# The scratch copy of queries and keys is laid out as the score stacks read it; neighbouring issues on the DMA queue are reordered

## The reference

```python
def reference(x, ...):                       # x: 8 images, 3 x 256 x 256
    gray = einsum('bchw,c->bhw', x, w)
    h = (|conv3x3(gray, scharr_x)| + |conv3x3(gray, scharr_y)|) / 2      # 8 x 256 x 256
    a = layernorm(h)                         # 8 images of 256 tokens of 256 values
    q, k, v = a@Wq+bq, a@Wk+bk, a@Wv+bv      # 16 heads of 16 values
    q, k = q@Wp, k@Wp                        # per head
    h = h + softmax(q k^T / 4) v             # per head
    n = layernorm(h); m = layernorm(n)*gamma + beta
    return h + n + 0.5*(silu(m@w1 + b1)@w2 + b2)     # w1: 256x1024, w2: 1024x256, dequantized
```

## Time and profile before

| | us |
|---|---|
| median of 3 runs (321.28, 323.62, 323.57) | 323.57 |
| the profiled execution | 326.8 |
| its span, first to last instruction | 325.1 |
| mean granted TensorE clock, share of 2.4 GHz | 0.958 |
| first stage on TensorE, until | 100.16 |
| second stage, first score by key | 104.49 |

### The profile page before, as it was taken

The page is one execution under the profiler, slowest core; times in us unless marked ns, Lnnn a source line. Parts: engine busy times, 40 slices in busy tenths (PEclk is TensorE's granted clock), DMA queues, the critical chain, the costliest instruction groups (busy, mean ns, idle before and its releaser), DMA issues.

```text
span 325.1 us, 5957 instructions
## 1 busy us (share of the span) xinstructions
PE 284.3 (87%) x2152; PEld 217.5 (67%) x2152; DVE 211.8 (65%) x421; ACT 165.7 (51%) x304; POOL 131.4 (40%) x250
## 2 busy tenths in 40 slices
PE   0599999999994999955998499879899999999996
PEld 0488888877773655533655265445699889999985
DVE  8979885947995699863699379661683563542422
ACT  1582524523331698853687379768434434444450
POOL 7533242402000058740396346217648769800000
PEclk9999999999999699995699879999999999999999
DMA  6939159671788812667064200000000100100101
GB/s 216 307 56 342 39 222 218 185 283 39 235 291 288 262 62 78 154 191 235 23 173 134 68 7 5 2 4 0 2 0 3 65 1 2 65 2 0 65 2 65
DMA packets 27215, 35.69 MB, mean 110 GB/s; under 512 B 5154, under 2 KB 16178, under 8 KB 27186
## 3 DMA queue, kind: packets, MB, share of 16 engines
q1 hardware_dynamic: 27024, 35.16, 36.1%
q10 hardware_dynamic: 162, 0.15, 0.2%
HBM read 24.42 MB, written 10.49 MB: 107 GB/s over the span
## 4 chain that ended last, share of the span: by engine, by line
PE 70%; DVE 13%; SPq 5%; DMA 4%; ACT 4%; issue 3%; ACTq 0%; DVEq 0%
PE bank L1160 42%; PE bank L1272 9%; PE bank L1252 8%; SPq L390 4%; PE bank L1230 4%; DMA qs<-negrow 3%; PE bank L1290 3%; ACT probs L1068 2%; DVE qk_l L857 2%; DVE negmax L867 1%; DVE gray L748 1%; PE bank L1298 1%; DVE xn L832 1%; PE bank L1182 1%; PE bank L1282 1%
## 5 line engine op out<-in xcount | busy, mean ns | idle before, releaser
L867 DVE TENSOR_REDUCE negmax<-bank 128x2 f32<-128x512 f32 x128 | 79.8, 683 | 26.2 <-PE bank L1230 26.1
L1068 ACT ACTIVATE probs<-bank 128x512 f32<-128x512 f32 x128 | 69.5, 595 | 39.0 <-PE bank L1252 35.9
L1252 PE MATMUL bank<-qs,ks 50*128 50x256 f32 x256 | 34.9, 354 | 21.0 <-DMA qs<-negrow 12.0
L921 DVE TENSOR_TENSOR y_l<-yf,y_h 128x512 fp32r<-128x512 f32 x32 | 23.6, 741 | 39.1 <-ACT yf L1094 39.0
L1091 ACT ACTIVATE y_h<-bank,b1col 128x512 fp32r<-128x512 f32 x32 | 22.0, 688 | 48.4 <-PE bank L1160 48.3
L1252 PEld LDWEIGHTS bank<-qs,ks 50*128 50x128 f32 x256 | 21.4, 206 | 34.9 <-DMA qs<-negrow 13.1
L1160 PE MATMUL bank<-w_h,y_h 128*128 128x256 f32 x128 | 36.9, 289 | 2.5 <-DVE y_l L921 2.1
L1272 PE MATMUL bank<-probs,vals 128*32 128x256 f32 x512 | 38.2, 421 | 0.0
L1160 PE MATMUL bank<-w_h,y_l 128*128 128x256 f32 x128 | 36.2, 282 | 0.0
L1160 PE MATMUL bank<-w_l,y_h 128*128 128x256 f32 x128 | 36.1, 282 | 0.0
L1230 PE MATMUL bank<-ks,qs 48*128 48x256 f32 x256 | 28.3, 319 | 1.6 <-DVE att L878 1.0
(11 more groups left out here) (143 smaller groups left out, 583.8 us busy)
## 6 DMA issues: line engine op xcount, KB each, us to landing
xr<-in_x SPq DMA_DIRECT2D x8, 768.0 KB, 8.2
qs<-qk_parts SPq DMA_DIRECT2D x48, 128.0 KB, 3.1
ks<-qk_parts SPq DMA_DIRECT2D x48, 128.0 KB, 3.3
qk_parts<-qk_h SPq DMA_DIRECT2D x16, 256.0 KB, 3.0
qk_parts<-qk_l SPq DMA_DIRECT2D x16, 256.0 KB, 3.0
wraw<-in_L_ffn_fc_q SPq DMA_DIRECT2D x4, 512.0 KB, 4.5
wscale<-in_L_ffn_fc_scales SPq DMA_DIRECT2D x4, 512.0 KB, 6.0
out<-osb SPq DMA_DIRECT2D x16, 128.0 KB, 1.8
```

The source lines that it names most:

```text
L867: eng.tensor_reduce(negmax[:, b % 2, u, v], entry_bank(key)[:, :].rearrange("p (t k) -> p t k", t=NT), AX.X, ALU.max, negate=True).then_in ...
L921: eng.tensor_tensor(y_l[:, p % 2, f], yf[:, n % 2], y_h[:, p % 2, f].bitcast(fp32), ALU.subtract).then_inc(s_y, 1)
L1068: eng.activation(probs[:, n % PBUF], p2[n % 3][:, :], ACT.Exp).then_inc(s_exp, 1)
L1252: ins = eng.matmul(p2[(n + v) % 3][:, t * N:(t + 1) * N], ks[rows, r, u, c + t * P:c + (t + 1) * P], qs[rows, r, u, c:c + N], start=True, ...
```

## The change

- `qk_dram` gets the shape [pair, op, part, m, v, d, u, t]. In the store the destination is walked as (u, v, d, t), 4 x 2 x 16 pieces of 2 KB, pieces of one u lying 8 KB apart; the source is 128 SBUF rows as before. In the load the source for one (m, v) is 16 rows of 8 KB, contiguous, and the destination 16 SBUF rows of 8 KB, contiguous in each row.
- `pass_neg(0, 0)` is issued ahead of all four stores of pair 3 instead of between the second and the third.
- Loads of pairs 2 and 3 are issued two a step over twelve steps (12 to 23, 28 to 39) instead of three a step over eight.
- The FFN weights of layer 1 are issued at steps 25 and 26 instead of 19 and 20, and `w2_step` and `normalise(0, .)` start three places later in `spare`: `w2_step` ends at step 44 instead of 40, `normalise(0, 5)` stands at step 52 instead of 48.

```diff
-    qk_dram = nc.dram_tensor("qk_parts", [PAIRS, 2, 2, E, COLS], fp32).ap()
+    qk_dram = nc.dram_tensor("qk_parts", [PAIRS, 2, 2, KE, 2, D, UNITS // KE, COLS], fp32).ap()
@@ store_qk
-                    eng.dma_start(qk_dram[p, op, part, m * P:(m + 1) * P, :], src[:, i, :].bitcast(fp32)).then_inc(s_store[i], 16)
+                    eng.dma_start(qk_dram[p, op, part, m].rearrange("v d u t -> u v d t"), src[:, i, :].bitcast(fp32)).then_inc(s_store[i], 16)
@@ load_qk
-                src = qk_dram[p, op, part, m * P:(m + 1) * P, :].rearrange("(u v d) t -> v d u t", v=2, d=D)[v]
-                eng.dma_start(dst[first:first + SPLIT - 2:3, r, m * 4:(m + 1) * 4, :].bitcast(fp32), src).then_inc(s_load[r][m], 16)
+                src = qk_dram[p, op, part, m, v].rearrange("d u t -> d (u t)")
+                eng.dma_start(dst[first:first + SPLIT - 2:3, r, m * 4:(m + 1) * 4, :].rearrange("p u t -> p (u t)").bitcast(fp32),
+                              src).then_inc(s_load[r][m], 16)
@@ SP, end of the first stage
+            pass_neg(0, 0)
             for i in range(4):
                 store_qk(3, i)
-                if i == 1:
-                    pass_neg(0, 0)
             pass_neg(0, 1)
@@ SP, the steps
-                    first = UNITS * (2 * p - 3) + 4
-                    for m in range(KE):
-                        k = s - first - 4 * m
-                        if 0 <= k < 4:
-                            if k == 0:
-                                stored(p, m)
-                            eng.wait_ge(s_p2, max(s, UNITS * (2 * p - 3) + 4 * (m + 1)))
-                            for i in range(3 * k, 3 * k + 3):
-                                load_qk(p, m, i)
-                if s in (19, 20):
-                    if s == 19:
+                    k = s - UNITS * (2 * p - 3) - 4
+                    if 0 <= k < 12:
+                        m = k // 6
+                        if k % 6 == 0:
+                            stored(p, m)
+                            eng.wait_ge(s_p2, s)
+                        for i in range(2 * (k % 6), 2 * (k % 6) + 2):
+                            load_qk(p, m, i)
+                        eng.wait_ge(s_p2, s)
+                if s in (25, 26):
+                    if s == 25:
                         eng.wait_ge(s_w1f, 2)
                     eng.wait_ge(s_p2, s)
-                    load_ffn(1, 2 * s - 38)
-                    load_ffn(1, 2 * s - 37)
+                    load_ffn(1, 2 * s - 50)
+                    load_ffn(1, 2 * s - 49)
@@ POOL
-                    elif 15 <= n < 27:
-                        w2_step(n - 15)
-                    elif 27 <= n < 33:
-                        normalise(0, n - 27)
+                    elif 18 <= n < 30:
+                        w2_step(n - 18)
+                    elif 30 <= n < 36:
+                        normalise(0, n - 30)
```

## The result

The changed kernel takes 352.05 us (median of 4, 349.27 to 353.91), the kernel before 323.6 beside it: ratio 1.0878, 95% interval 1.0773 to 1.0982. The forecast was 347.5 (332 to 368), slower. Ratios are formed from the fast executions of both kernels, since some executions of a kernel run in a slower state. The profiled execution took 350.96, its span is 349.2; before they were 326.8 and 325.1.

The account below looks back on a forecast made before the run. TensorE carried 70% of the chain of waits, SP's issuing and DMAs 5% and 4%. Step 4 +38.4, slow clock +3.7 and spacing -18.2 gave +23.9 on the profiled 326.8; as median 347.5 us, range 332 to 368.

Parts of the forecast that it names:

- Four engines for a store: First stage: every store runs on the same 4 engines instead of 16, DMA share 0.25; chance 0.80 as summed.
- The rival of sixteen engines: First stage: stores split by the source's 128 rows and cost what they did; 299 to 307 us, chance 0.10.
- The price of a store: First stage: a store on four engines takes 2.7 us (2.6 to 2.8) at 23.7 GB/s an engine, against 0.65 before.
- the quick rival: First stage: four engines, each faster than 23.7 GB/s, break-even at 34 GB/s; 315 to 333 us, chance 0.04.
- The price of a load: First stage: a load of 8 KB on each of its 16 engines takes 0.45 us (0.33 to 0.64).
- no gap in between: First stage: the four engines start about 42 and carry stores, loads and negated rows without a pause.
- The chain: First stage: queued stores and loads land the second negated rows at 151, delaying step 4 by 38.4 us.
- Its issue time: SP, first stage: issuing a load or store changes by some tenths of 0.64 us, off the path.
- The slow clock after step 4: TensorE after step 4's wait of over 10 us: low clock for the next steps, +3.7 us.
- The spacing: Second stage: two loads a step and later weights remove 12.0 us of waits plus slow clock, -18.2 in all (bound -12).
- the spacing is wrong: Sign, second stage: a wait of TensorE for negated rows that stays after step 8 would refute the spacing.
- worse than summed: Rival: SP blocked in stores, late loads at its pace of 0.64, +9; 363 us, up to 375; chance 0.06.

Follow-up runs that it names:

- e_pitch: Kernel 2: the kernel before with rows of the DRAM copy 8 KB apart, 2 KB used of each, outermost dimension still 128; 326.7 us, ratio 1.0029.
- e_pad4: Kernel 1: the kernel before with an unused row behind each 32 rows of the DRAM copy, so the store's destination has outer count 4; 364.44 us, ratio 1.1184.
- e_layout: Kernel 4: the kernel before with only the changed DRAM tensor, store and load, and the order of before on every queue; 363.48 us, ratio 1.1164.
- e_pad8: Kernel 3: the kernel before with an unused row behind each 16 rows of the DRAM copy, outer count 8; 334.94 us, ratio 1.0279.
- Kernels 8 and 9: 8: e_perm with second-stage negated rows passed a step later, 310.62 us; 9: 8 with layer 1's weight DMAs one a step at steps 24 to 27, 310.05 us.
- e_perm: Kernel 7: the changed kernel with weight columns permuted so that the store is contiguous, loads still in 8 KB pieces; 310.76 us, ratio 0.9566.

## Why the prediction was right

**The mechanism.** Four engines for a store was read from a row with 8 rows against 2, and held for 128 against 4; kernels 1 to 3 show that the outer count of the destination alone sets it, 4, 8 and 128 rows giving 4, 8 and 16 engines (shares 0.26, 0.51, 1.04), and that nothing of the time hangs on the scattered addresses. The traces count the same: the semaphore of a store is updated 16 times in the kernel before and in e_pitch, but 5 times in the changed kernel, e_pad4 and e_layout and 9 times in e_pad8, the first of them 0.4 us after the end of the issue, the other 4 or 8 when data lands. The rule of the Trainium skill (page "DMA: Bandwidth & Descriptors", section on why a DMA increments its semaphore by 16) agrees at all three. The rival of sixteen engines is out.

**The price of a store.** 2.7 us was taken; 256 KB at 102 GB/s are 2.57, and the high parts show it too: from (2, 0) to (2, 3), 83.35 to 98.83, six stores landed, 2.58 each. By the share that is 102 / (16 x 0.26) = 24.5 GB/s for an engine, against the 23.7 of the forecast. That it would go at 34 was the quick rival; it doesn't.

**The price of a load.** 0.45 on each engine. Between the landings at 66.92 and 83.35 lie 24 loads and two stores, (16.43 - 5.14) / 24 = 0.47 each; between 98.83 and 108.30 twelve and two, 0.36; and from 123.72 to step 4 at 149.39 twelve loads and eight stores, 0.34 with 1 us for the landing. That is 19.7 for the 48 instead of 21.6.

**The start.** Here "no gap in between" failed. Store (0, 3) landed at 66.92, and eight stores of 2.57 back from there is 46.4, not 42: in the window from 42 to 46 the stores moved only 36 GB/s. Two stores, 5.1 us of work for four engines, were issued by 42.99, so it was not for want of work; why they began slowly is open.

**The chain.** Step 4: forecast 151, measured 149.4, that is 4.4 for the start, -4.2 for 32 stores and -1.8 for the loads. Release of `qk_high(2, 3)`: 96 and 98.8, of `qk_high(3, 3)`: 123 and 123.7; the late start shows in the first, and the store term, a little too high, has made up for it by the second. Step 0, 129.5 and 129.4, agrees by luck. The forecast let it wait over 20 us for the negated rows, and no such wait is there (the one it expected before step 4, over 10 us, is: 13.91). The rows landed at 128.3, while TensorE was at pair 3's last products, which it had got late because ScalarE and VectorE waited for stores: the path of `qk_high(3, 3)` and not that of the rows. The two came 1.1 us apart. The sum went by step 4 and did not need it. That the earlier `pass_neg(0, 0)` spares the rows 21.6 was a slip, too: before, it stood behind four of the eight stores, which is 10.8, and kernel 4 has step 0 only 7.7 later.

**SP.** Its issue time was called off the path. It is on it: SP's issuing is 17% of the chain, for a slow store holds SP as well.

**The slow clock after step 4.** Forecast +3.7, measured +1.75: the clock is low from 149.6 (0.55 in the mean to 155), but at its upper level by step 8, not by step 10.

**The spacing.** This is the term that was mis-sized: I took "all of it", -18.2, and it gave -14.6. The long waits went, 12.0 us, and with them the slow stretches; but waits of 1.57, 0.43 (loads, steps 26 and 42) and 1.17 (rows, step 32) came in their place. The last is also the sign that the forecast had named for "the spacing is wrong", a wait for negated rows behind step 8; it is a sixth of the longest before, so the spacing works, but not in full. My count of SP's time had 2 x 0.64 a step for loads, and 1.36 for rows once in four; together that is 1.6 a step against 1.54, so SP does fall behind while loads are issued, and I had written both that it "no longer falls behind" and that it is late "by a microsecond or two". Kernels 8 and 9 show that it is more than SP: with the wait for loads nearly gone (0.16), the rows of step 32 still waited, behind 2 MB of weights.

**Taken together:** 36.8 + 1.75 - 14.6 + 0.2 = 24.1 against 23.9. The errors of -1.6, -1.9 and +3.6 cancelled; the sum is better than its terms. Of the rival "worse than summed", its first half was seen (SP blocked at 2.4 us a store), its price was not: the loads that SP issued late cost the four engines 0.34 to 0.47 each and not its pace of 0.64. The twelve behind pair 2's stores were all issued by 122.4, before the last of these stores had landed (123.7).

## What to carry to other kernels

Before a DMA gets a new shape, look at the outermost dimension of both sides: here 2, 4 and 8 on the shorter side gave 2, 4 and 8 engines and 128 gave all sixteen, so a layout that made the loads' pieces long and contiguous took three quarters of the stores' bandwidth. If the order of the rows is the trouble, permute the producer (here the columns of a small weight matrix) and leave both transfers contiguous. A change of several parts is worth taking apart even if it is clearly slower: here a gain of 4.3% was hidden in a loss of 8.8%.

## What the runs showed of the hardware

- The rate of an engine hardly depends on how many work: 102, 195 and 394 GB/s for stores on 4, 8 and 16 engines are 25.5, 24.4 and 24.6 GB/s each (by the busy share, 0.26, 0.51 and 1.04, they are 24.5, 23.9 and 23.7).
- A load of 128 KB as 16 pieces of 8 KB costs SP 0.589 us (median of 48), as 64 pieces of 2 KB 0.595, and lands in 3.4 to 3.5 us against 3.1 to 3.3; with stores on 16 engines (e_perm) 8 KB pieces landed in 3.2 to 3.4. Going from 2 KB to 8 KB did nothing for these loads.
- Writes of 2 KB pieces 8 KB apart go at 394 GB/s, as contiguous ones do.
- SP isn't free of a slow DMA that it has issued: with stores on four engines it stands still in the issue from the fourth to sixth store of a group on, 2.4 us each (on eight engines 1.2), and all that is queued behind waits, loads on sixteen engines too (the first load behind pair 2's stores took 2.76 us to issue).
